# Fewer semaphore waits on every engine, and a buffer of turned q and k for each item of a pair

## The reference, cut to what matters

```python
for i in range(6):
    x = attn_layer(shift_tokens(x), Wqkv[i], q_scale[i], k_scale[i], Wo[i]) + x
    x = ffn_layer(shift_tokens(x), ln_g[i], ln_b[i], W1[i], b1[i], W2[i], b2[i]) + x

def attn_layer(x, Wqkv, qs, ksc, Wo):              # 16 heads of 64, INNER = 1024
    q, k, v = split(x @ Wqkv)                      # by head
    q, k = l2norm(q) * qs, l2norm(k) * ksc         # then rotary, with scales
    sim = q k^T * 8 in windows of 32 queries and 64 keys, masked
    return softmax(sim) v @ Wo

def ffn_layer(x, ...):                             # DIM_INNER = 341
    a, gate = split(norm(x) @ W1 + b1)
    return a * gelu(gate) @ W2 + b2
```

## Time and profile before

| what | value |
|---|---|
| median of 3 runs | 1468.31 us (1467.17 to 1468.71) |
| span of the profiled execution | 1465.0 us |
| PE busy | 1387.9 us, 95% |
| PEld busy | 1111.8 us, 76% |
| DVE busy | 1295.4 us, 88% |
| ACT busy | 1268.8 us, 87% |
| POOL busy | 1182.8 us, 81% |

### The profile page before, as it was taken

One profiled execution on the slowest core, in us unless ns is written; L12 is line 12 of the kernel. 1 busy time (PEld: TensorE's weight loads), 2 busy tenths in 40 slices (PEclk: granted clock), 3 DMA queues, 4 the chain that ended last, 5 costly groups with the idle time before them and its releaser, 6 DMA issues.

```text
span 1465.0 us, 79260 instructions
## 1 busy us (share of the span) xinstructions
PE 1387.9 (95%) x30176; PEld 1111.8 (76%) x30176; DVE 1295.4 (88%) x2400; ACT 1268.8 (87%) x2523; POOL 1182.8 (81%) x1162
## 2 busy tenths in 40 slices
PE   6689999999999999999999999999999999999996
PEld 4467877777787777777778777777877777787874
DVE  5678999999999999999999999999999989999972
ACT  5578998999999899989999998999999888889883
POOL 2587888888888888888888888888888878888860
PEclk9789999999999999999999999999999999999997
DMA  5211111121211122121122111113111112111111
GB/s 142 84 49 49 36 50 47 45 83 40 56 35 50 50 56 73 35 56 35 50 59 70 49 39 53 37 48 94 35 43 37 35 31 82 43 29 43 37 36 30
DMA packets 61752, 75.09 MB, mean 51 GB/s; under 512 B 8462, under 2 KB 35340, under 8 KB 61708
## 3 DMA queue, kind: packets, MB, share of 16 engines
q1 hardware_dynamic: 61708, 74.51, 18.6%
HBM read 18.90 MB, written 1.05 MB: 14 GB/s over the span
## 4 chain that ended last, share of the span: by engine, by line
PE 90%; issue 3%; DVE 1%; POOL 1%; ACT 0%; POOLq 0%; DVEq 0%; ACTq 0%
PE bank L1181 13%; PE bank L1168 12%; PE bank L1271 12%; PE bank L1261 10%; PE bank L1221 10%; PE bank L1169 9%; PE bank L1170 9%; PE bank L1306 4%; PE bank L1295 4%; PE bank L1297 2%; PE bank L1296 2%; PE bank L1285 2%; PE bank L1279 1%; POOL P L446 0%; POOL u L440 0%
## 5 line engine op out<-in xcount | busy, mean ns | idle before, releaser
L426 POOL TENSOR_TENSOR u<-u,t 128x512 f32<-128x512 f32 x384 | 489.6, 1281 | 88.1 <-DVE t L910 76.6
L440 POOL TENSOR_TENSOR u<-u,rn 128x512 f32<-128x512 f32 x384 | 388.6, 1044 | 0.0
L612 ACT ACTIVATE sq<-bank 128x512 f32<-128x512 f32 x384 | 231.7, 604 | 70.6 <-PE bank L1170 68.7
L1168 PE MATMUL bank<-Wl,xsh 128*128 (+1 forms) x576 | 265.5, 461 | 15.8 <-POOL xsl L420 7.2
L446 POOL TENSOR_TENSOR P<-P,rs 128x512 f32<-128x512 f32 x192 | 196.4, 1044 | 103.6 <-DVE rs L938 103.6
L910 DVE TENSOR_TENSOR t<-bank,TS 128x512 f32<-128x512 f32 x384 | 258.5, 683 | 5.8 <-ACT sq L612 1.8
L894 DVE TENSOR_REDUCE ss<-sq 128x8 f32<-128x512 f32 x384 | 255.7, 676 | 6.9 <-issue 6.3
L901 DVE TENSOR_TENSOR u<-bank,TC 128x512 f32<-128x512 f32 x384 | 255.0, 674 | 1.6 <-ACT sq L612 1.6
L637 ACT COPY qkT<-bank 128x512 f32<-128x512 f32 x384 | 221.5, 593 | 13.1 <-PE bank L1181 5.7
L1169 PE MATMUL bank<-Wh,xsl 128*128 (+1 forms) x576 | 229.0, 398 | 0.0
L1170 PE MATMUL bank<-Wh,xsh 128*128 (+1 forms) x576 | 228.6, 397 | 0.0
(11 more groups left out here) (92 smaller groups left out, 2743.2 us busy)
## 6 DMA issues: line engine op xcount, KB each, us to landing
vs<-v SPq DMA_DIRECT2D x384, 128.0 KB, 2.3
Wraw<-in_L_ffn_Wqkv_dram SPq DMA_DIRECT2D x72, 117.5 KB, 2.2
WoS<-in_L_ffn_Wo_dram SPq DMA_DIRECT2D x6, 512.0 KB, 4.1
W1h<-Wh SPq DMA_DIRECT2D x6, 341.0 KB, 2.6
W1l<-Wl SPq DMA_DIRECT2D x6, 341.0 KB, 2.9
Wraw<-in_L_ffn_W_dram SPq DMA_DIRECT2D x12, 116.0 KB, 2.2
out_dram<-X SPq DMA_DIRECT2D x4, 256.0 KB, 2.3
W2S<-in_L_ffn_W_dram SPq DMA_DIRECT2D x6, 128.0 KB
```

The costliest lines, as they stand in the source:

```text
L426: nc.gpsimd.tensor_tensor(u[:, r, c], u[:, r, c], t2[:, r, c % 2], ALU.add).then_inc(add_done[c], 1)
L440: nc.gpsimd.tensor_tensor(by_head(u[:, r, c]), by_head(u[:, r, c]), spread(rn[:, r, HC * c:HC * c + HC], HC, DH), ALU.mult).then_inc(qk_re ...
L1168: nc.tensor.matmul(out, x[0], Wl[:, w], start=True, stop=False)
```

## The change

Waits are dropped where another wait of the same step, or an earlier step on the same queue, already covers them. Which of several results comes last is written down in small tables by item (`chunk_read`, `heads_turned`, `heads_normal`, `P_divided` and so on). `qkT` gets a dimension for the item. The order of the steps is the same on every engine. The rewritten loop of SP issues the same transfers in the same order, and the functions that are only renamed are left out below.

```diff
-        qkT = sb("qkT", [128, 2, 2, 4, 128])
+        qkT = sb("qkT", [128, 2, 2, 2, 4, 128])
...
-        FREED = {"chunk": lambda k: [sq_done[k], rot_done[k], t2_done[k]],
+        FREED = {"chunk": lambda k, r: [chunk_read[k][r]],
...
-        HEADS_BACK = [[1, 0], [1, 0], [1, 0], [1, 0]]
+
+        chunk_read = [[rot_done[0], rot_done[0]], [t2_done[1], t2_done[1]], [t2_done[2], rot_done[2]], [rot_done[3], t2_done[3]]]
+        squares_done = [ss_done[2], ss_done[2]]
+        heads_normal = [[qk_ready[0], qk_ready[1]], [qk_ready[3], qk_ready[2]]]
+        all_normal = [qk_ready[3], qk_ready[1]]
+        heads_turned = [[qk_out[1], qk_out[0]], [qk_out[3], qk_out[3]]]
+        scores_seeded = [seeded[0], seeded[0]]
+        scores_full = [sc_full[1], sc_full[0]]
+        P_divided = [P_ready[1], P_ready[0]]
+        P_copied = [PT_ready[0], PT_ready[0]]
...
                 def add(c, lag, r):
                     n = (it - lag) * 2 + r
-                    pool.wait_ge(rot_done[c], n_(n) + 1)
-                    pool.wait_ge(t2_done[c], n_(n) + 1)
+                    pool.wait_ge(chunk_read[c][r], n_(n) + 1)
...
                 def bound_norms(lag, r):
                     n = (it - lag) * 2 + r
-                    for c in range(NCH):
-                        pool.wait_ge(ss_done[c], n_(n) + 1)
+                    pool.wait_ge(squares_done[r], n_(n) + 1)
...
                     act.wait_ge(qk_turned[s], n_(n) + 1)
-                    act.wait_ge(sc_full[s], n_((it - lag - HEADS_BACK[k][r]) * 2 + 1 - r) + 1)
-                    nc.scalar.copy(qkT[:, s].rearrange("p w t (g i) -> p (w t) g i", g=2)[:, :, g],
+                    act.wait_ge(sc_full[s], n_(n) - 1)
+                    nc.scalar.copy(qkT[:, r, s].rearrange("p w t (g i) -> p (w t) g i", g=2)[:, :, g],
...
-                    dve.wait_ge(sum_done[0], n_(n) + 1)
-                    dve.wait_ge(sum_done[1], n_(n) + 1)
+                    dve.wait_ge(sums_full[r], n_(n) + 1)
...
-                def chunk(c, lag, r):
-                    n = (it - lag) * 2 + r
+                def parts_ready(lag):
                     pe.wait_ge(W_split, (it - lag) // LAYER_PAIRS * LAYER_PAIRS + LAYER_PAIRS + START)
                     pe.wait_ge(xs_split, n_(it - lag) + 1)
+
+                def chunk(c, lag, r):
                     freed(lag, "chunk", c, r)
...
-                    pe.wait_ge(W_split, (it - lag) // LAYER_PAIRS * LAYER_PAIRS + LAYER_PAIRS + START)
-                    pe.wait_ge(xs_split, n_(it - lag) + 1)
                     freed(lag, "v", j, r)
...
+                def seeds_ready(lag, r):
+                    pe.wait_ge(scores_seeded[r], n_((it - lag) * 2 + r) + 1)
+
                 def scores(s, lag, r):
                     n = (it - lag) * 2 + r
-                    pe.wait_ge(seeded[0], n_(n) + 1)
-                    pe.wait_ge(seeded[1], n_(n) + 1)
-                    pe.wait_ge(qk_out[2 * s], n_(n) + 1)
-                    pe.wait_ge(qk_out[2 * s + 1], n_(n) + 1)
+                    pe.wait_ge(heads_turned[s][r], n_(n) + 1)
...
                 def turn_p(lag, r):
                     n = (it - lag) * 2 + r
-                    pe.wait_ge(P_ready[0], n_(n) + 1)
-                    pe.wait_ge(P_ready[1], n_(n) + 1)
+                    pe.wait_ge(P_divided[r], n_(n) + 1)
...
                 def up(j, lag):
                     pair = it - lag
-                    pe.wait_ge(xf_ready, n_(pair) + 1)
-                    pe.wait_ge(w1_loaded, pair // LAYER_PAIRS * 32 + 32 + START)
+                    if j == up_first:
+                        pe.wait_ge(xf_ready, n_(pair) + 1)
+                        pe.wait_ge(w1_loaded, pair // LAYER_PAIRS * 32 + 32 + START)
```

More of the change, by code:

```diff
@@ L101, in program @@
         qT4 = [t2[:, g // 2, g % 2] for g in range(GROUPS)]
-        vT4 = [qkT[:, g // 2, g % 2].rearrange("p t n -> p (t n)") for g in range(GROUPS)]
+        vT4 = [qkT[:, 0, g // 2, g % 2].rearrange("p t n -> p (t n)") for g in range(GROUPS)]
         v4 = [PT[:, g // 2, g % 2] for g in range(GROUPS)]
@@ L198, in program @@
         OF_PAIR = ("Wo", "xc", "up", "down")
-        FREED = {"chunk": lambda k: [sq_done[k], rot_done[k], t2_done[k]],
[L200 to L208, removed]
+        FREED = {"chunk": lambda k, r: [chunk_read[k][r]],
+                 "v": lambda k, r: [v_ready[k]],
+                 "turn_qk": lambda k, r: [qk_out[k]],
+                 "scores": lambda k, r: [sc_out[k]],
+                 "turn_p": lambda k, r: [PT_ready[k]],
+                 "values": lambda k, r: [OT_ready[k]],
+                 "Wo": lambda k, r: [res_done],
+                 "xc": lambda k, r: [xf_ready],
+                 "up": lambda k, r: [[gelu_done], [hh_ready], [hh_ready]][k],
+                 "down": lambda k, r: [h_ready]}
         BANK_USERS = [
@@ L251, in bank_left @@
                     if other in OF_PAIR:
-                        return [(s, n_(before + (LAYER_PAIRS if s is h_ready else 0)) + 1) for s in FREED[other](ok)]
-                    return [(s, n_(before * 2 + orr) + 1) for s in FREED[other](ok)]
+                        return [(s, n_(before + (LAYER_PAIRS if s is h_ready else 0)) + 1) for s in FREED[other](ok, orr)]
+                    return [(s, n_(before * 2 + orr) + 1) for s in FREED[other](ok, orr)]
             return []
@@ L382, in _, with values_of, block_of, next_layer @@
             place_up(0)
-            for it in range(PAIRS + LAST + 1):
[L384 to L395, removed]
+            def values_of(it, lag, r):
+                if 0 <= it - lag < PAIRS:
+                    shifted_values((it - lag) * 2 + r)
+            def block_of(it, lag):
+                if 0 <= it - lag < L * NB // 2 - 3 * RAW_SLOTS:
+                    load_block(it - lag + 3 * RAW_SLOTS)
+            def next_layer(it, lag, load):
+                pair = it - lag + 1
+                if 0 < pair < PAIRS and pair % LAYER_PAIRS == 0:
+                    load(pair // LAYER_PAIRS)
+            for it in range(PAIRS + LAST + 1):
+                values_of(it, 1, 1)
+                next_layer(it, 2, load_out)
+                block_of(it, 0)
+                next_layer(it, 2, place_up)
+                next_layer(it, 2, load_down)
+                values_of(it, 0, 0)
             for q in range(4):
@@ L619, in norms @@
                     act.wait_ge(ln_done, n_(n) + 1)
-                    for c in range(NCH):
-                        act.wait_ge(qk_ready[c], n_(n) - 1)
+                    act.wait_ge(all_normal[r], n_(n) - 1)
                     act.sem_inc(wait_met, 1)
@@ L707, in split_high @@
                     act.wait_ge(raw_loaded, pair * 32 + 32 * (NB // 2 + 1))
[L708 to L710 removed]
+                    act.wait_ge(x_read, n_(pair * 2) - 1 + x_read_of)
                     act.wait_ge(w1_loaded, pair // LAYER_PAIRS * 32 + START)
@@ L1223, in scores @@
                                                                     at:at + (32 if w == 0 else 64)],
-                                            qkT[f, s, 0, t, 32 * w:32 * w + 32], qkT[f, s, 1, t, seen], start=False,
+                                            qkT[f, r, s, 0, t, 32 * w:32 * w + 32], qkT[f, r, s, 1, t, seen], start=False,
                                             stop=True, skip_group_check=True)
```

32 lines of the change are left out of this document (15 added, 17 removed).

## The result

The changed kernel takes 1453.43 us (median of 4 runs, 1450.53 to 1456.63) against 1467.74 for the kernel before (median of 4, 1466.32 to 1468.71): a ratio of 0.9896, 95% interval 0.9875 to 0.9917 (the two medians divide to 0.9903; the ratio on record is used throughout). The forecast was 1452. The total agrees, but its parts do not: the turn gained less than the sum said, and the rest of the difference lies outside the repeated turn.

A forecast was written before the change was run, and what follows sets the result against it. PE, busy for 95% of the span, was taken to bound the kernel, losing time to wait instructions. 0.15 + 0.10 + 0.13 - 0.02 = 0.36 us a turn, times 45, is 16.2 us: about 1452 us, range 1445 to 1463.

The forecast's parts named there:

- A: PE's `turn_p` of item 1 directly behind `turn_qk`: two wait instructions fewer gain 0.15 us a turn.
- B: Second `scores` call of item 0 on PE: one wait instruction fewer gains 0.10 us a turn.
- C: `down` and `chunk(1, 0, 1)`: fewer POOL waits ahead of `norms` make ACT and its followers earlier, 0.13 us a turn.
- D: Path from `variance` to `up`: no wait dropped there, PE only idles longer ahead of `up`; gain 0.
- E: Other waits dropped on PE, ACT, DVE and SP are hidden behind work; gain 0, ends 0 and 0.05 us.
- rival 1: Taken back: ACT and POOL paths have less room; 0.13 to 0.25 us a turn, 1457 to 1462 us; chance 0.25.
- F: Second buffer of `qkT`: the stall it is meant for isn't there; gain 0.
- G: PE reaches `chunk(3, 0, 0)` earlier and there needs POOL's `x_rest`, which just suffices; 0.02 us a turn taken off.
- the prediction's own sign of being wrong: Loop turn staying above 28.2 us, with PE waiting at `x_rest`, the copy ahead of `turn_qk` or `gated`.
- the 45: Turns of the loop, about 45 of 48, for which the gain of 0.36 us was taken to hold: 16.2 us.

The follow-up runs named there:

- e2: Changed kernel with the old waits of `turn_p` and its banks put back; ratio 0.9991 to the kernel before, turn 28.393 us.
- e3: Changed kernel with the old waits of `scores` put back ahead of each call; ratio 0.9959 to the kernel before, turn 28.300 us.
- e5: Kernel before with waits thinned only in `turn_p` of item 1 and the second `scores` call of item 0; ratio 0.9917, turn 28.114 us.
- e9: Changed kernel with the two waits swapped in four ACT and DVE steps between `variance` and `up`; ratio 0.9896 to the kernel before, turn 28.107 us.
- e10: Changed kernel with the two waits of `p_out` alone in the other order; ratio 0.9874 to the kernel before, turn 28.068 us.
- e1: Kernel before with the new buffer dimension of `qkT` alone, no wait thinned; ratio 1.0005, turn 28.422 us.
- e12: Changed kernel run once more, nothing altered; ratio 0.9910 to the kernel before, turn 28.164 us.
- e4: Changed kernel with the two waits of `norms` in the other order; ratio 0.9916 to the kernel before, turn 28.163 us.
- e8: Changed kernel with the two waits swapped in nearly every ACT and DVE step and POOL's `bound_norms`; ratio 0.9867 to the kernel before, turn 27.982 us.

## Why the prediction was right, and where not

The total was right for a partly wrong reason, and its closeness is luck: the turn gave little over half of what was forecast, and what lay outside it made up the rest. By its own terms, in a turn:

- A: forecast 0.15, measured 0.16 between the groups. Right, and e2 shows that nothing else stands in for it.
- B: forecast 0.10, measured 0.11 (e3: 0.12). Right. The Trainium skill's "Advanced Engine Details and Errata" gives TensorE a queue of 64 under "Engine Queue Depths", and under "Sequencer Loop" it lets further instructions be read and queued meanwhile. That this hides a wait behind short matmuls, and makes B nothing, was the prediction's inference from it; the 0.11 us of B speak against the inference.
- C: forecast 0.13, measured about 0.02. This is the step that failed: "ACT, DVE's `gated` and `o_out` come that much earlier". From `up` to the second matmul behind `down` it is 7.64 us before and 7.62 now (medians). POOL gained 0.08 and not 0.12, and ACT's `norms` lost it again on a register instruction that moved under its wait. The second matmul behind `down` still starts 0.34 us after the first. I had compared the waits of each step in the built program, and not which instruction each of them rides on.
- D: forecast 0, measured about 0 (from `variance` to `up` the time is 0.03 us less, which e5 has in part as well, and the loads idle for 0.48 us). The prediction saw an engine working or a result just arrived at each point of the path; e9 shows that it has 0.07 us of the queue's own in it, which this change leaves alone.
- E: forecast 0 and wrong by a loss. The waits that stayed were packed anew, and `values` behind `p_out` comes 0.08 us later (e5), which another order of its waits gives back (e10). No term had it, though rival 1 had the form of it, a copy by ACT that PE waits for.
- F: forecast 0, and e1 gives no change in the time. Its turn is 0.04 us longer, little more than the scatter, for a cause that wasn't tried.
- G: forecast -0.02. Between `scores` and the product of `chunk(3, 0, 0)` nothing changed: the distance from the start of the last `scores` matmul to it is 0.47 us before and 0.46 now, medians over the turns.

0.16 + 0.11 + 0.02 - 0.08 = 0.21, and the turn shows 0.20, against 0.36. That is within rival 1's 0.13 to 0.25 us a turn, and in part its mechanism: C stayed out, as it said, but A and B were both kept, and the loss is at `p_out` and not at `x_rest` or the copy ahead of `turn_qk`. The turn of 28.178 is just short of the prediction's own sign of being wrong, 28.2. Rival 1's 1457 to 1462 us did not come, since the start, the first turns and the last ones gave 5.9 us that no case of mine had.

Where these 5.9 us come from stays open. The stalls of new code don't explain them: the four over 0.9 us add up to 6.3 us in the profile before (1.97, 1.98, 1.24, 1.13) and to 7.3 in the changed one (2.59, 1.17, 1.76, 1.81), though the one of 1.24 us ahead of 1186.50 is gone. And e5 has nothing of the kind: 47 turns of 0.264 are 12.4 us, and its ratio gives 12.2. Nor can a single profile split it. The span less 47 turns is 131.3 us before, 125.3 in the changed kernel and 127.0 in its second profile, e12; among the kernels that differ from the changed one only in the order of some waits off PE (e4, e8, e9, e10) it goes from 121.9 to 130.2. I treated the 3 of 48 turns outside the 45 as if they gave nothing, which left no room for any of this.

## What to carry to other kernels

Where a busy engine's queue has short work back to back, each instruction in it that isn't work costs about 0.1 us, and taking it away gains that, but only there: two places of this change gave all the gain, and the rest cost 0.06 us a turn as it was written. (Once the late waits were ordered, the rest gave up to 0.075.) After every such edit look at the waits that stay: which of them is late, and whether the instruction that needs it carries it directly, with the number it compares with already in a register. Writing the waits in another order gave here as much as taking so many away, 0.20 us a turn.

And judge by the turn of the loop, not by the median alone, when the code's length changes: the first pass through new code has stalls of its own that move with every instruction.

## What the runs showed of the hardware

- On PE's queue a semaphore instruction takes 0.106 us and a register instruction 0.092 from its start to the next one's, by the records ahead of `turn_p` in the kernel before and in e1, two to three times what their own rows show (0.051 and 0.032). At the start of the program the same semaphore instruction came every 0.15 us.
- On ACT POOL's late result reached the activation of `norms` in 0.03 us where the wait rode on it (the kernel before, e1), in 0.09 through a semaphore instruction (e4, e8) and in 0.11 through a register instruction (the changed kernel).
- In code run for the first time PE stood for 0.9 to 2.8 us at places 256 instructions apart in its queue (not at all of them), and these places moved with instructions put ahead of them.
- The granted clock stayed at 1.00 in the loop with PE idle for 0.85 us a turn.
